# A mixture-of-experts kernel on one core: the routing chain is remade, and the norms and the split of x move to GpSimd

## What is computed

```python
def ffn(x):                       # E = 64 experts, F = 64, top 8 of 64
    shared = silu(xf @ Ws_up) @ Ws_down
    aff = xf @ centroids.T
    _, idx = top_k(aff + expert_biases, 8)
    w = sigmoid(take_along_axis(aff, idx, axis=1))
    w = w / (sum(w, axis=-1, keepdims=True) + 1e-08)
    cw = zeros((T, E)).at[arange(T)[:, None], idx].add(w)
    h = silu(einsum('td,edf->etf', xf, W_up))
    y = einsum('etf,efd->etd', h, W_down)
    return shared + einsum('etd,te->td', y, cw)

def attn(u):                      # no attention matrix: a gated mix of two projections
    xf = concatenate([u[:, :1], u[:, 1:] @ WB.T], axis=1)
    xb = concatenate([u[:, 1:] @ WBf.T, u[:, -1:]], axis=1)
    gamma = sigmoid(xf @ w1.T + xb @ w2.T + b)
    return gamma * (xf + xb) + (1.0 - gamma) * u

x = x + 0.5 * ffn(layernorm(x))
x = x + attn(layernorm(x))
x = x + 0.5 * ffn(layernorm(x))
```

## Time and profile before

| | |
|---|---|
| time before, median of 3 runs | 836.47 us (836.36 to 836.81) |
| span of the profiled execution, first to last instruction | 834.9 us |
| median of the runs less this span | 1.57 us |
| PE busy | 809.7 us (97% of the span), 3691 matmuls |
| DVE, ACT, POOL busy | 698.6, 654.2, 404.6 us (84%, 78%, 48%) |
| DMA, mean over the span | 14 GB/s |

### The profile page before, as it was taken

One profiled execution on the slowest core, in us unless ns is written; L12 is line 12 of the kernel. 1 busy time (PEld: TensorE's weight loads), 2 busy tenths in 40 slices (PEclk: granted clock), 3 DMA queues, 4 the chain that ended last, 5 costly groups with the idle time before them and its releaser, 6 DMA issues.

```text
span 834.9 us, 12478 instructions
## 1 busy us (share of the span) xinstructions
PE 809.7 (97%) x3691; PEld 648.0 (78%) x3691; DVE 698.6 (84%) x1456; ACT 654.2 (78%) x1204; POOL 404.6 (48%) x355
## 2 busy tenths in 40 slices
PE   7899999999999999999999999999999999999998
PEld 5777778877778777787777877778778787788786
DVE  7998888798887988879888798787896987888875
ACT  5886679778787787877878788786878868876975
POOL 2764545544445444554545455354453644544443
PEclk9999999999999999999999999999999999999999
DMA  7000000000000000000000000000000000000000
GB/s 264 20 1 26 1 1 1 1 13 14 13 1 1 25 0 13 0 0 25 0 13 0 0 25 0 13 0 0 25 0 0 0 0 27 0 1 1 14 0 13
DMA packets 16046, 11.51 MB, mean 14 GB/s; under 512 B 1680, under 2 KB 14992, under 8 KB 16016
## 3 DMA queue, kind: packets, MB, share of 16 engines
q1 hardware_dynamic: 16016, 11.15, 4.2%
HBM read 9.05 MB, written 2.10 MB: 13 GB/s over the span
## 4 chain that ended last, share of the span: by engine, by line
PE 47%; DVE 18%; issue 15%; POOL 11%; ACT 7%; DMA 0%; POOLq 0%; DVEq 0%; ACTq 0%
POOL g_lo L351 8%; PE up L700 7%; PE up L701 7%; PE up L702 7%; PE y_ps L700 7%; PE y_ps L702 7%; PE y_ps L701 7%; DVE g_lo L578 3%; DVE up L569 3%; DVE gated L569 3%; DVE normed L515 2%; PE side L709 2%; ACT up L410 2%; ACT g_hi L418 2%; POOL rstd L341 2%
## 5 line engine op out<-in xcount | busy, mean ns | idle before, releaser
L351 POOL TENSOR_TENSOR g_lo<-gated,g_hi 128x512 fp32r<-128x512 f32 x256 | 332.3, 1298 | 370.9 <-ACT g_hi L418 370.3
L410 ACT ACTIVATE up<-up 128x512 f32<-128x512 f32 x528 | 310.9, 590 | 74.7 <-PE up L702 73.3
L569 DVE TENSOR_TENSOR gated<-up,cw 128x512 f32<-128x512 f32 x256 | 174.7, 682 | 51.6 <-ACT up L410 47.7
L569 DVE TENSOR_TENSOR up<-up,cw 128x512 f32<-128x512 f32 x256 | 175.9, 687 | 48.8 <-ACT up L410 45.5
L700 PE MATMUL up<-x_hi,wu_hi 128*128 128x512 f32 x512 | 204.3, 399 | 7.2 <-DVE g_lo L578 7.2
L700 PE MATMUL y_ps<-g_hi,wd_hi 128*128 128x512 f32 x512 | 208.4, 407 | 1.7 <-POOL g_lo L351 1.7
L702 PE MATMUL y_ps<-g_hi,wd_lo 128*128 128x512 f32 x512 | 202.4, 395 | 0.0
L701 PE MATMUL up<-x_lo,wu_hi 128*128 128x512 f32 x512 | 202.2, 395 | 0.0
L702 PE MATMUL up<-x_hi,wu_lo 128*128 128x512 f32 x512 | 201.9, 394 | 0.0
L701 PE MATMUL y_ps<-g_lo,wd_hi 128*128 128x512 f32 x512 | 201.8, 394 | 0.0
L418 ACT CAST g_hi<-gated 128x512 fp32r<-128x512 f32 x256 | 157.7, 616 | 48.1 <-DVE gated L569 45.8
(11 more groups left out here) (100 smaller groups left out, 564.1 us busy)
## 6 DMA issues: line engine op xcount, KB each, us to landing
x_in<-in_x SPq DMA_DIRECT2D x8, 256.0 KB, 2.7
wu_raw<-in_w_up SPq DMA_DIRECT2D x4, 512.0 KB, 5.8
wd_raw<-in_w_down SPq DMA_DIRECT2D x4, 512.0 KB, 6.8
x_res<-in_x SPq DMA_DIRECT2D x8, 256.0 KB, 2.7
out<-out_sb SPq DMA_DIRECT2D x7, 256.0 KB, 2.2
out<-out_sb SPq DMA_DIRECT2D x2, 128.0 KB, 1.8
sm_raw<-in_ident SPq DMA_DIRECT2D x2, 64.0 KB, 5.2
ident<-in_ident SPq DMA_DIRECT2D x1, 64.0 KB, 2.6
```

The costliest lines, as they stand in the source:

```text
L351: nc.gpsimd.tensor_tensor(g_lo[:, i, :], gated[:, t // 2 % ORING, :], g_hi[:, i, :].bitcast(fp32), ALU.subtract).then_inc(lo_done[1], 1)
L410: nc.scalar.activation(up[i][:, :], up[i][:, :], ACT.Silu).then_inc(silu_done, 1)
L569: nc.vector.tensor_tensor(gated[:, t // 2 % ORING, :] if t % 2 else up[i][:, :], up[i][:, :], cw[ph.q][:, :], ALU.mult).then_inc(gate_done, 1)
```

## The change

- **Affinities.** `aff` was fp32r in two parts (two matmuls for each of four blocks, with the centroids split into `ce_both`, and a sum of the halves on DVE). It is now one plain fp32 matmul for each block, of 64 columns, from an fp32 copy of the turned x (`x_raw`, made by ACT in the place of `x_hi`). `aff` and the sigmoid's result stay in PSUM, beside each other in `side1`. `aff_sum` and `eps` are gone (the 1e-8 is a 65th column of `w_sel`).
- **x.** `x_hi` and `x_lo` are both made on POOL from `x_raw` (`x_split`: a copy and a subtraction), except for the first two, which DVE makes.
- **Norms.** The four blocks of `norm` are made on POOL behind `rstd`, except for those of the first two rows' inputs.
- **Slots.** All tables are rewritten. `max`, `take`, `gate`, `sum` and `inv` stand in the sigmoid's slot or the next. The norm ahead of the second expert layer is made within the B stage (slot 23) and no longer at the start of the A stage (slots 2 and 4).
- `t1` is written back into PSUM in place; the weights are laid out so that the duplication of the routing weights (`w_out`) has the experts innermost; the early part of `cw` ahead of the third and the last phase (`late`) is gone.

```diff
 AT_STEADY_A = {
-    "x_t": 7, "x_hi": 8, "x_lo": 10, "aff": 13, "aff_sum": 14, "sig": 15, "bias": 16, "max": 18, "take": 20,
-    "gate": 22, "sum": 24, "eps": 26, "inv": 27, "cw": 28, "cw_t": 31, "cw_copy": 32,
-    "y_t": 6,
-    "stat0": (12, 14), "aggr0": 16, "rstd0": 17, "norm0": (28, 30),
-    "aggr2": 0, "rstd2": 1, "norm2": (2, 4),
-    "y": 2, "out": 8, "keep": 11,
+    "x_t": 3, "x_copy": 3, "x_split": 5, "aff": 7, "bias": 8, "sig": 9, "max": 9, "take": 9,
+    "gate": 9, "sum": 9, "inv": 9, "cw": 11, "cw_t": 20, "cw_copy": 20,
+    "y": 2, "y_t": 5, "out": 6, "keep": 13,
+    "stat0": (14, 16), "aggr0": 18, "rstd0": 19, "norm0": 21,
 }
 AT_STEADY_B = {
-    "x_t": 1, "x_hi": 2, "x_lo": 4, "aff": 8, "aff_sum": 8, "sig": 9, "bias": 10, "max": 14, "take": 15,
-    "gate": 17, "sum": 19, "eps": 20, "inv": 21, "cw": 22, "cw_t": 26, "cw_copy": 26,
-    "y_t": 6, "x1": 8, "stat1": (10, 12), "aggr1": 13, "rstd1": 14, "norm1": (16, 18), "xu": 19, "u_t": 22,
-    "u_copy": 23, "attn": 28, "tanh": 29, "gamma": 30, "t1": 30, "x2": (32, 33),
-    "stat2": (34, 34),
-    "y": 2,
+    "x_t": 1, "x_copy": 1, "x_split": 3, "aff": 4, "bias": 4, "sig": 5, "max": 5, "take": 5,
+    "gate": 5, "sum": 5, "inv": 5, "cw": 7, "cw_t": 11, "cw_copy": 11,
+    "y": 2, "y_t": 5, "x1": 6, "stat1": (7, 8), "aggr1": 8, "rstd1": 9, "norm1": 9, "xu": 11, "u_t": 14,
+    "u_copy": 14, "attn": 17, "tanh": 17, "gamma": 17, "t1": 18, "x2": (19, 20),
+    "stat2": (21, 22), "aggr2": 22, "rstd2": 23, "norm2": 23,
...
+            def norm(k, c):
+                hold(pool, rstd_done[k], c + 1)
+                for n in range(NB):
+                    made = nc.gpsimd.tensor_scalar(normed[k][:, n, :], norm_from[k][:, n, :], mv[k][:, n, 0:1],
+                                                   rstd[k][:, n:n + 1], ALU.subtract, ALU.mult)
+                made.then_inc(norm_done[k], 1)
+
+            def x_split(q, n):
+                hold(pool, x_copied[q], n + 1)
+                nc.gpsimd.tensor_copy(x_hi[q][:, :], x_raw[:, :]).then_inc(x_hi_done[q], 1)
+                pool.wait_ge(x_hi_done[q], n + 1)
+                nc.gpsimd.tensor_tensor(x_lo[q][:, :], x_raw[:, :], x_hi[q][:, :].bitcast(fp32),
+                                        ALU.subtract).then_inc(x_lo_done[q], 1)
...
             def sigmoid(q, n):
-                act.wait_ge(aff_summed[q], n + 1)
-                nc.scalar.activation(sig[:, :, :], aff[:, :, :], ACT.Sigmoid).then_inc(sig_done[q], 1)
+
+                act.wait_ge(bias_done[q], n + 1)
+                nc.scalar.activation(sig, aff, ACT.Sigmoid).then_inc(sig_done[q], 1)
...
             def affinities(q, n):
-                pe.wait_ge(x_lo_done[q], n + 1)
-
+                pe.wait_ge(x_copied[q], n + 1)
                 for m in range(NB):
-                    nc.tensor.matmul(rows(side1, m), rows(x_hi[q], m), ce_both[:, :], start=True, stop=False)
-                    last = nc.tensor.matmul(side1[:, m * P:m * P + E], rows(x_lo[q], m), ce_both[:, 0:E], start=False, stop=True)
+                    last = nc.tensor.matmul(aff[:, m, :], rows(x_raw, m), ce_raw[:, :], start=True, stop=True)
                 last.then_inc(aff_done[q], 1)
```

More of the change, by code:

```diff
@@ L59 @@
 AT_FIRST = {
[L60 to L62 removed]
+    "x_t": 9, "x_copy": 10, "x_split": 11, "aff": 12, "bias": 12, "sig": 17, "max": 18, "take": 19,
+    "gate": 20, "sum": 21, "inv": 21, "cw": 23, "cw_t": 33, "cw_copy": 33,
+    "stat0": (1, 2), "aggr0": 3, "rstd0": 3, "norm0": 5,
     "v": 11, "v_copy": 14, "wu_hi": (None, None, 2, 5, 8, 12, 15, 20),
@@ L67 @@
 }
[L68 to L75, removed]
+AT_MID_PREP = {
+    "y": 2, "y_t": 5, "x1": 6, "stat1": (7, 8), "aggr1": 8, "rstd1": 9, "norm1": 9, "xu": 11, "u_t": 12,
+    "u_copy": 12, "attn": 15, "tanh": 15, "gamma": 15, "t1": 16, "x2": (17, 18),
+    "stat2": (19, 20), "aggr2": 20, "rstd2": 21, "norm2": 21,
+    "x_t": 24, "x_copy": 24, "x_split": 25, "aff": 27, "bias": 27, "sig": 28, "max": 28, "take": 28,
+    "gate": 29, "sum": 29, "inv": 29, "cw": 31, "cw_t": 33, "cw_copy": 33,
+}
@@ L76 @@
+AT_SECOND = AT_MID_PREP | {
+    "stat0": (22, 23), "aggr0": 24, "rstd0": 27, "norm0": 27, "keep": 23,
 }
 AT_THIRD = {
[L78 to L81 removed]
@@ L82 @@
-    "stat2": (34, 34),
-    "late": 3,
+    "x_t": 4, "x_copy": 4, "x_split": 5, "aff": 7, "bias": 8, "sig": 9, "max": 9, "take": 9,
+    "gate": 9, "sum": 9, "inv": 9, "cw": 11, "cw_t": 13, "cw_copy": 13,
+    "y": 2, "y_t": 5, "x1": 6, "stat1": (7, 8), "aggr1": 8, "rstd1": 9, "norm1": 9, "xu": 13, "u_t": 16,
+    "u_copy": 16, "attn": 19, "tanh": 19, "gamma": 19, "t1": 20, "x2": (21, 22),
+    "stat2": (23, 24), "aggr2": 24, "rstd2": 25, "norm2": 25,
 }
 AT_STEADY_A = {
-    "x_t": 7, "x_hi": 8, "x_lo": 10, "aff": 13, "aff_sum": 14, "sig": 15, "bias": 16, "max": 18, "take": 20,
@@ L619, in phase @@
                             aggr(k, c)
-                        blocks, last = halves(ph, f"norm{k}", t)
-                        if blocks:
-                            norm(k, c, blocks, last)
-                    for name, step in (("x_lo", x_low), ("aff_sum", sum_aff), ("bias", add_bias), ("max", find_top), ("take", take_top),
-                                       ("gate", select), ("sum", sum_up), ("eps", add_eps), ("inv", invert)):
+                    if ph.first and ph.at["norm0"] == t:
+                        early_norm(1)
+                    if ph.first and ph.at["x_split"] == t:
+                        early_x_split(q)
+                    for name, step in (("bias", add_bias), ("max", find_top), ("take", take_top),
+                                       ("gate", select), ("sum", sum_up), ("inv", invert)):
                         if ph.at.get(name) == t:
```

144 lines of the change are left out of this document (61 added, 83 removed).

## The result

The changed kernel takes 848.73 us (median of 4 runs, 847.71 to 849.62), the kernel before 836.57 beside it on the same chip. The ratio is 1.0145, with a 95% interval of 1.0130 to 1.0159. The prediction said 823.1, with 812 to 831 as its range, and gave 0.09 to slower: it was wrong, on the other side of no change. The span of the profiled execution grew from 834.9 to 846.2.

A forecast was written before the change was run, and what follows sets the result against it. PE's matmul cadence was taken as the limit, with only its 20.7 us of waits to win. Terms -10.8 (A stages), +1.0 (B stages) and -3.6 (starting and last phases) sum to -13.4: 836.47 to 823.1 us, range 812 to 831.

The forecast's parts named there:

- A stage, 6 x 1.8 gained: Six A stages: waits for the norm, routing weights and up bank go, 1.8 us each, 10.8 in all.
- 0.1 for misfits and 0.3 for ACT: A stage: 0.1 us left for misfits; PE's demand for the up bank estimated 0.3 earlier because ACT is later.
- the rival that saw the stall made again there: A stage: the routing burst ends 0.5 later than ACT, eleven stages lose 0.5 to 0.7 more; 830 us, chance 0.15.
- bias behind the table loads: Up bank: without DVE's bias addition there, the low part would end at T + 5.9 instead of T + 7.0, without PE waiting.
- Affinities, 0: Affinities: four plain fp32 matmuls a phase cost 0.9 us, as now, so gain 0; at most 7 us if 64 columns were cheaper.
- Bias near 420 ns: DVE's bias addition, 1095 ns on average before, was expected to fall to near 420 ns.
- DVE below 640 us: DVE's total busy time was expected to fall below 640 us, as a sign of the prediction holding.
- x_split, 0: Making x_hi and x_lo on POOL costs PE 0, up to 0.5 us a stage if the cover is gone.
- B stage, +0.2 each: Five B stages: up-bank wait shrinks, a new wait for POOL's low part comes; +0.2 us each, 1.0 in all.
- I take the middle, 420: Norm block on POOL, not in the trace: 420 ns taken between 350 and 520, so four blocks are 1.7 us.
- third rival: B stage, slot 9: the norm on POOL is slow, 1.3 us a block, +17.6 in five stages; 841 us, chance 0.10.
- Starting and last phases, -3.6: Three starting and last two phases: 60% of 5.9 us of old waits goes, gaining 3.6, between 0 and 5.9.

The follow-up runs named there:

- e5: The kernel before with the bias addition one slot earlier, in the sigmoid's slot, in steady A and B stages; 826.50 us, ratio 0.9878.
- e12: e5 with, in the A stage, the second half of the norm of x2 a slot earlier and the turn of x and what follows a slot later; 824.32 us.
- e8: The changed kernel with POOL's norm blocks as one multiplication by rstd, the mean's subtraction left out; 835.50 us, ratio 0.9993.
- e1: The changed kernel with the norms back on DVE in halves, one and two slots behind rstd; 848.92 us, ratio 1.0146.
- e9: The changed kernel with POOL's norm as two operations over 128x512 in place of four blocks; 834.74 us, ratio 0.9977.
- e2: The changed kernel, tables alone changed: turns PE waited at two to four slots later, some routing weights turned in the next phase; 843.34 us, ratio 1.0089.
- e6: The changed kernel with norms on DVE in halves and the turns of u and x two to five slots later; 822.35 us, ratio 0.9829.
- e4: The kernel before with only the norm blocks moved to POOL, each at the slot of its first half; 862.42 us, ratio 1.0312.
- e10: e9 with later turns, POOL's norm behind an odd tile's low part, and the second stage's norm for the next row moved to slot 18; 818.33 us.

## Why the prediction was wrong, step by step

*A stage, 6 x 1.8 gained: right, and more.* 2.3 each. No wait of PE is left there, and the prediction's 0.1 for misfits and 0.3 for ACT weren't needed. The five routing steps lie in the table loads' gap as it said: in the B stage the sigmoid's table load begins at T = 438.17, max at 438.97 and the reciprocal at 441.61, and the next gating follows at 441.76, T + 3.6, where the prediction had T + 3.6. So the rival that saw the stall made again there fell. e5 shows that the step behind this term, bias behind the table loads, was the right one. e5 and e12 also show that 1.5 of the 2.3 need none of the changed work.

*Affinities, 0: right.* Eight matmuls a phase, 1.00 us with the last one's latency. *Bias near 420 ns:* 414. *DVE below 640 us:* 616.7. *x_split, 0:* right, no wait of PE for it in the steady stages.

*B stage, +0.2 each: wrong, by the size of one number.* The step was "I take the middle, 420". A block took 800 ns. The working drew a line by elements through a 4-element instruction and 128x512 ones (350 to 520), as if the form of the instruction didn't matter, and used the ends of that line as bounds, in spite of rstd's 1051 ns for four elements, which stood in the same rows. The 1.45 us more a norm give 1.6 more a stage than forecast, because there are two norms in it and PE has two places to wait at, the turn of u and the low part behind. The sum had no term for the turn (it was taken to be late enough) and none for the norm of x2. At 420 ns a block both would have been nothing: of the 1.92 lost around the first norm about 0.5 would be left, and the 0.51 behind the second would be gone, an estimate that takes 1.45 off each. So here the mechanism was right, and the mis-sized term is the block. The third rival named the mechanism and the place, and priced it with 1.1 us a block as the point from which it decides. That point counted one norm a stage, 20 blocks; with both norms it is 0.42 + 13.4 / 40 = 0.76, below the 0.80 measured. In e8, at 2.4 us a norm or 0.6 a block, the kernel is already level with the one before.

*Starting and last phases, -3.6: wrong, the largest error.* They gave +15.7. The step that failed was "their turn stands only three to four slots later, so a part comes back. I take 60%": a share of the old waits, with no chain worked out, and so bounded by nothing and 5.9 on the gaining side alone. The chain would have been there to add up, and so would the tables, which put the turns of u and x two to three slots earlier than before and not later. In the second to last stage the aggregation ends and POOL starts var_eps at 747.43; 0.3 + 1.1 + 3.15 us later the norm is there, and PE stood at its turn from 749.8 on. With the assumed 420 ns a block it would still have waited 0.8. The routing chain's waits, 2.1 to 2.5 us idle, three times, don't depend on the norm: they are in all of e1, e8 and e9. e2 and e6, with later turns, bring the second to last stage to 50.9 and 50.3, so for that stage the place of the turns is shown to be the cause.

*The clock was no term.* Behind the first wait of 2.27 us in these stages 1.6 us are lost at the lower level.

*The rule named against the move* (the Trainium skill, GPSIMD Engine Reference, Engine selection: elementwise work on GpSimd takes about twice VectorE's time with two inputs) was weighed and given only the third rival's chance of 0.10. Here a norm takes 3.15 us on POOL against four times 588 ns on DVE, 2.35, so the ratio is 1.3. (A block has one tensor and two scalar columns as inputs, so it isn't the rule's two-input case.) What decided is not the ratio but the place: PE's turn stood right behind the norm, and low parts for which PE waits were queued behind it. In the A stage, and in the B stages of e4, the same norm of 3.15 us cost nothing: rstd and a low part are made well ahead of it there. Which of these distances does it was not tried by itself.

*The whole.* What would a norm of 1.7 us with the change's tables have taken? No run has it. An estimate: each of five B stages loses 2.0 less, and each of the second and second to last 2.9 less in two waits and 1.6 less in the slow stretch; together 19 us, so about 830. The block's price is then some 19 of the 25.6 us by which the forecast was off, and the early turns and the routing weights of the second, third and second to last stage are the rest, less the 3 us that the A stages won beyond the forecast. 830 would have lain in the stated range, but 823 not within reach; e9, at 2.1 us a norm, is the nearest run, 831.7 at its fastest.

## What to carry to other kernels

Price a moved operation by a row of the same form, or by none: an instruction with a scalar a partition isn't a piece of a wider one with two tensors. When the price has no row, ask what stands behind the moved work in its new queue, and who waits for its result; try it behind what is urgent instead of ahead (e4's B stages have a norm of 3.14 us in such a place and lose nothing by it; e10 did the same with a shorter norm and later turns). Do the stages at the start and end chain by chain as well: here six A stages won 13.5 us, and three stages that run once gave 15.7 back. And before work is moved to relieve an engine, try what other slots of the table give: two numbers gave 1.2% here.
